# One state in eight takes its input product from GpSimd and its decay from PSUM; in the last batches four states take theirs from TensorE, and TensorE's sums move behind tiles and fills

## The reference

```
dt = softplus(x_ssm @ dt_w + dt_b);  A = -exp(A_log);  B = x_ssm @ Bp;  C = x_ssm @ Cp
state = state * exp(dt * A) + (dt * x_ssm) * B      # for every time step, channel and state
y = sum over the states of state * C                # then the D term, the gate silu(z) and Wout
```

## Time and profile before

| | us |
|---|---|
| median of the runs | 1844.28 |
| the profiled execution | 1847.7 |
| its span | 1845.9 |
| VectorE busy | 1725.2 |
| TensorE busy (modelled) | 1589.4 |
| GpSimd busy | 1371.3 |
| ScalarE busy | 1360.6 |

### The profile page before, as it was taken

One profiled execution on the slowest core, in us unless ns is written; L12 is line 12 of the kernel. 1 busy time (PEld: TensorE's weight loads), 2 busy tenths in 40 slices (PEclk: granted clock), 3 DMA queues, 4 the chain that ended last, 5 costly groups with the idle time before them and its releaser, 6 DMA issues.

```text
span 1845.9 us, 42152 instructions
## 1 busy us (share of the span) xinstructions
PE 1589.4 (86%) x12756; PEld 790.5 (43%) x12756; DVE 1725.2 (93%) x1913; ACT 1360.6 (74%) x2504; POOL 1371.3 (74%) x675
## 2 busy tenths in 40 slices
PE   1778659999999999999999999988988889888887
PEld 1544334444444444444444444443434334443343
DVE  6798559999999999999999999999999999999996
ACT  3476748878777868787878777787777687687871
POOL 5036547777777768776777777778989899888985
PEclk9688769999999999999999999999899999899998
DMA  8435565556555665567554655575456555545542
GB/s 236 148 124 187 169 161 119 127 125 175 132 126 125 150 151 126 124 146 169 120 125 125 176 125 126 124 160 129 95 120 146 138 121 103 125 118 130 129 88 64
DMA packets 202208, 249.44 MB, mean 135 GB/s; under 512 B 25939, under 2 KB 104221, under 8 KB 201949
## 3 DMA queue, kind: packets, MB, share of 16 engines
q1 hardware_dynamic: 198020, 239.78, 54.2%
q0 software_dynamic: 4096, 8.40, 1.5%
HBM read 204.00 MB, written 43.66 MB: 134 GB/s over the span
## 4 chain that ended last, share of the span: by engine, by line
PE 29%; issue 25%; DVE 20%; POOL 13%; DMA 5%; ACT 4%; DVEq 2%; SPq 1%; POOLq 0%; ACTq 0%
DVE arena L1151 11%; POOL arena L663 10%; PE ps L1329 10%; PE ps L1343 8%; DVE ps L1141 7%; DMA x_rms_by_expert<-arena,slots 4%; PE ps L1417 2%; ACT arena L883 2%; PE ps L1315 2%; POOL x_rms_by_expert L630 2%; PE ps L1393 1%; SPq L328 1%; POOL pick L587 1%; ACT arena L889 1%; DMA u_scratch<-arena 1%
## 5 line engine op out<-in xcount | busy, mean ns | idle before, releaser
L663 POOL TENSOR_TENSOR arena<-arena 128x1024 f32<-128x1024 f32 x512 | 1202.7, 2362 | 322.3 <-DVE arena L1151 286.3
L1151 DVE TENSOR_TENSOR_SCAN arena<-arena,ps 128x512 f32<-128x512 f32 x1024 | 1176.1, 1201 | 54.7 <-PE ps L1329 37.8
L883 ACT ACTIVATE arena<-arena,neg_A 128x512 f32<-128x512 f32 (+1 forms) x1024 | 671.7, 713 | 87.6 <-DVE arena L1151 86.8
L1343 PE MATMUL ps<-arena,ident 64*64 64x512 f32 x4096 | 569.4, 628 | 3.0 <-POOL arena L663 2.8
L1329 PE MATMUL ps<-arena 128*64 128x128 f32 x6144 | 437.8, 287 | 128.7 <-DVE arena L1151 119.5
L1329 PEld LDWEIGHTS ps<-arena 128*64 128x64 f32 x6144 | 342.2, 141 | 448.8 <-DVE arena L1151 286.6
L1141 DVE TENSOR_TENSOR ps<-arena,ps 128x512 f32<-128x512 f32 x640 | 406.0, 680 | 7.1 <-PE ps L1315 6.4
L889 ACT ACTIVATE arena<-ident,b_turned 128x128 f32<-128x128 f32 x768 | 242.7, 388 | 0.0
L1343 PEld LDWEIGHTS ps<-arena,ident 64*64 64x64 f32 x4096 | 110.6, 134 | 160.2 <-issue 160.2
L630 POOL DMA_INDIRECT x_rms_by_expert<-arena,slots x64 | 69.9, 1091 | 127.6 <-DVE slots L1096 89.2
L1315 PE MATMUL ps<-b_parts,pick 120*128 120x512 bf16 x320 | 124.0, 387 | 13.0 <-DVE arena L1151 12.5
(11 more groups left out here) (166 smaller groups left out, 957.1 us busy)
## 6 DMA issues: line engine op xcount, KB each, us to landing
arena<-c_scratch SPq DMA_DIRECT2D x128, 1024.0 KB, 8.7
arena<-w_routed_scaled SPq DMA_DIRECT2D x40, 256.0 KB, 5.9
arena<-in_L_ffn_W_r_dram SPq DMA_DIRECT2D x40, 256.0 KB, 8.5
arena<-w_shared_tiles SPq DMA_DIRECT2D x128, 64.0 KB, 8.0
x_rms_by_expert<-arena SPq DMA_DIRECT2D x1, 5120.0 KB, 22.4
arena<-x_rms_by_expert SPq DMA_DIRECT2D x40, 128.0 KB, 7.2
routed_by_expert<-arena SPq DMA_DIRECT2D x40, 128.0 KB, 8.3
sz_scratch<-arena SPq DMA_DIRECT2D x8, 512.0 KB, 4.6
```

Of the source, the lines that this page charges most:

```text
L663: nc.gpsimd.tensor_tensor(products[:, i % RING, :, :], states[:, i % 2, :, :], c_rows[:, i // CG, i % CG, :].unsqueeze(1).broadcast_to((P, ...
L883: nc.scalar.activation(decay[:, 2 * i + h, :], dflat[:, ds(slot + h * L, L)], ACT.Exp, scale=aflat[:, ds(col, 1)]).then_inc(s["decay_ready ...
L1151: vector.tensor_tensor_scan(states[:, i % 2, h, :], decay[:, m, :], ps[bank][:], 0.0, ALU.mult, ALU.add).then_inc(s["scanned"], 1)
L1343: ins = mm(y_ps[r][HP * h:HP * h + HP, :], ident[q, q], products[q, slot, h, :], start=False, stop=False, skip_group_check=True)
```

## The change

- `KIND` becomes a pair: DEDDEDEP for block groups, DEDDEDEE for the others. State 6 changes from D to E in both. State 7 is of a new kind P in block groups and stays E in the others. Both have four D states instead of five.
- A P state: GpSimd computes u*B into SBUF with one operation of 128x1024, issued after the product of state 1, from a row of B that a new DMA broadcasts to all partitions (256 KB, `b_row`). ScalarE writes the state's two decays into the two PSUM banks, in the slots of its order that belong to states 5 and 6; all other decays keep their place. The scan then has its decay in PSUM and u*B in SBUF.
- In the last batches a fourth state needs diagonal copies by ScalarE and fills by TensorE.
- In every slot of TensorE's queue the second fill moves behind the tiles and other work of the slot, and the sum moves behind the second fill.
- The two matmuls that open the expert sum in a batch's head are gone; the first expert matmul starts the sum. They now stand in the seven final groups (`begin_final`) and in the last group, with DMAs for xn and the gates.
- `pick` keeps one column per row of B (96x32 instead of 120x5120), and the matmul reads it with a broadcast step of 0. The projection of C and B has 128 output rows instead of 104.

The diff, cut to its core:

```
-    KIND = "DEDDEDDE"
+    KIND = ("DEDDEDEE", "DEDDEDEP")
+    P_AT = SG - 1
...
-        pick = sb("pick", [3 * SQ, SQ, P], BF16)
+        pick = sb("pick", [3 * SQ, SQ], BF16)
...
+        u_b = products[:, RING]
...
+            def load_b_row(u, g, tb):
+                if not isinstance(u, int) or u:
+                    sp.wait_ge(s["u_b_pooled"], u)
+                sp.dma_start(b_row, c_d[S:C_B_ROWS][ds(g, 1), ds(tb, L)].broadcast_to((P, L))).then_inc(s["b_row_loaded"], 16)
...
                 load_w1_shared(u, g)
                 if block:
+                    load_b_row(u, g, tb)
                     e = expert_of(u)
                     load_x_rows(u)
...
+                    if blocks and i == 1:
+                        pool.wait_ge(s["dt_u_loaded"], b * 32 + 32)
+                        pool.wait_ge(s["b_row_loaded"], (b * E + g) * 16 + 16)
+                        nc.gpsimd.tensor_tensor(
+                            u_b, u_in.rearrange("p n h t -> p (n h t)")[:, ds(slot, NH * L)].rearrange(
+                                "p (h t) -> p h t", h=NH),
+                            b_row.unsqueeze(1).broadcast_to((P, NH, L)), ALU.mult).then_inc(s["u_b_pooled"], 1)
...
+            def decay_to_psum(u, g, slot, h):
+                col = snap(g * SG + (h * S + P_AT))
+                nc.scalar.activation(ps[BANKS[True][P_AT][h]][:], dflat[:, ds(slot + h * L, L)], ACT.Exp,
+                                     scale=aflat[:, ds(col, 1)]).then_inc(s["p_decay_ready"], 1)
...
                         act.wait_ge(s["scanned"], m0 + (2 * i + h + 1))
+                        if block_before and (i, h) in ((P_AT - 2, 1), (P_AT - 1, 0)):
+                            decay_to_psum(*before, 1 - h)
+                        if KIND[block][i] == "P":
+                            continue
...
+                        if KIND[block][i] == "P":
+                            dve.wait_ge(s["u_b_pooled"], u + 1)
+                            dve.wait_ge(s["p_decay_ready"], u * NH + (h + 1))
+                            vector.tensor_tensor_scan(states[:, i % 2, h, :], ps[bank][:], u_b[:, h, :], 0.0,
+                                                      ALU.mult, ALU.add).then_inc(s["scanned"], 1)
+                            continue
...
-            def open_ffn(b, odd):
-                pe.wait_ge(s["open_loaded"], b * (16 * N_OPEN) + 16 * N_OPEN)
-                pe.wait_ge(s["xn_loaded"], max(b * 16 + 16, 32))
-                mm(ffn_ps[:], ident[:], xn_in[:, odd, :], start=True, stop=False)
-                mm(ffn_ps[:], b2_sb[:], gates_in[:], start=False, stop=False).then_inc(s["sums_opened"], 1)
+            def add_xn_b2(bank, xn):
+                mm(bank[:], ident[:], xn, start=False, stop=False, skip_group_check=True)
+                mm(bank[:], b2_sb[:], gates_in[:], start=False, stop=False, skip_group_check=True)
...
-                    for k in (HEAD_SUM_AT if head else SUM_AT).get(i, ()):
-                        if k >= 0 or not head or last is not None:
-                            ysum(n0, k)
-                    if ahead and KIND[ahead[1]] == "E":
-                        fill(*ahead, ahead_odd, 1)
                     if block:
                         if first and i == FIRST_X_AT:
                             turn_x(u)
...
+                    if ahead and KIND[ahead[3]][ahead[1]] == "E":
+                        fill(*ahead, ahead_odd, 1)
+                    for k in (HEAD_SUM_AT if head else SUM_AT).get(i, ()):
+                        if k >= 0 or not head or last is not None:
+                            ysum(n0, k)
```

215 lines of the change are left out of this document (126 added, 89 removed).

## The result

| | before | after |
|---|---|---|
| median of the runs made together, us | 1845.7 | 1834.2 |
| span of the profiled execution, us | 1845.9 | 1833.4 |
| ratio, 95% interval | | 0.9947 (0.9935 to 0.996) |

The change makes the kernel 11.5 us faster by the medians; by the ratio it is 0.5%. The forecast was 30 us faster. The time lies inside the range of 1795 to 1840 and outside the likeliest case's own of 1800 to 1829.

What follows compares the result with a forecast made beforehand. VectorE, busy 93% of the span, was taken as the bound. Gains of 12 + 15 + 2.3 + 0 + 0.8 = 30 us took 1844.3 to 1814 us, with an 8-in-10 range of 1795 to 1840.

Steps and rivals of the forecast that it cites:

- likeliest case: Whole kernel: forecast of 1814 us, own range 1800 to 1829, chance 0.73.
- GpSimd's waits in block groups: Thirty middle block groups: waits of 0.35 at states 4 and 7, group 23.89 to 23.5, 12 us gained.
- Batch 0: First two groups of batch 0: 3.4 us shorter, with 0.5 more than other batches for its longer wait.
- state P's decay is late: Rival: ScalarE's second PSUM decay comes late, 1.5 to 2 us in 40 groups; 1878 us at 1.6; chance 0.06.
- The constants: Start to first scan: smaller `pick` lets SP's stores go some 4 us earlier, VectorE's first scan 2.3 us earlier.
- the 2.29 go: Preamble: VectorE's 2.29 us wait for the scaled weights disappears, and no more than that is gained.
- Heads and second groups of batches 1 to 4: Heads 0.6 us shorter and second groups 2.3 shorter per batch; 11.6 us gained over these four batches.
- The last three batches: Final groups wait 1.5 to 2 us, six groups behind them 1.7; sum 0, between -15 and +20 us.
- The clock: TensorE behind new waits: throttled clock costs some 2 us in each of six groups, making the sum 12 us higher.
- At the end: Last group: one pair of multiplications less, 0.8 us gained after its wait.
- the last batches take it back: Rival: final groups cost 2 us more and the clock falls behind new waits, 26 us, giving 1840; chance 0.12.

Runs made afterwards that it cites:

- the third buffer: The changed kernel with a third state buffer, so scans of states 2 to 7 wait for products one state further back: 1784.8 us, ratio 0.9674.
- Another order on ScalarE: The changed kernel with group 0's P decays behind group 1's decays of states 0 and 1 and state 1's diagonal copies: 1828.3 us, ratio 0.991.
- the kernel before with the small `pick`: The kernel before with a third state buffer and `pick` cut to 40 columns: 1845.0 us, ratio 0.999.
- the one with the new order: The kernel before with only TensorE's sums and second fill moved behind each slot's other work, the fill first: 1863.2 us, ratio 1.01.
- the changed kernel with the wait last: The changed kernel with VectorE's wait for GpSimd's product placed last, directly before the state's first scan: 1819.2 us, ratio 0.9873.

## Why the prediction was wrong

**GpSimd's waits in block groups: the step that failed most (8.4 us of the missing 17.5).** The places, states 4 and 7, and the cause, the product of two states back, were right. The sizes weren't: "it waits 0.35" counted from the product's end to the scan without the instructions that stand between the wait and the scan in a loop, 0.2 us at each place. With them out of the way the waits were 0.37 and 0.25 and the group 23.40, against 23.5 forecast. The 0.1 for GpSimd's ninth operation wasn't needed: u*B takes 2.37 and its successor follows at once (744.97 to 747.29 for u*B and the start of product 2). With a group that gains 0.4 when all goes well, 0.2 twice is the whole of it. (In full, against the third buffer's 22.57: the two waits and the overlap that they lose cost 1.20, where the forecast had 0.8 with its 0.1; and a group without them is 22.57, not 22.7, because the pair of multiplications ahead of state 2 takes 1.17 instead of 1.30.) The larger miss is what the gain hung on: the forecast named the two state buffers as a rule of the code, took the two waits as a given and put no price on a third buffer, which was worth 50 us.

**Batch 0 (5.8 us).** The forecast gave its head the saving of the other heads. It had the rival "state P's decay is late" and looked for it in the loop, where the decays were in time (the second ended at 758.15, for a scan at 759.4). It wasn't worked out for the first group, where ScalarE comes out of the gelus 32 us into the group with a whole group of decays ahead of the P decays: 6.85 us. So the first group got 6.6 us longer (40.43 to 47.05, forecast 0.6 shorter), and the second 4.3 shorter (28.03 to 23.76, forecast 2.8): it waited for fills before, as the earlier trace rows show in a later batch, and waits for none now. Another order on ScalarE gets 3.2 back.

**The constants (2.8 us).** Two steps failed. GpSimd's selections did fall from 18.66 us to 0.91, and SP issued the zeros 5.2 us earlier (22.30 against 27.48), but "the 2.29 go" didn't happen: the wait is 2.42. The zeros landed no earlier (49.86 against 49.92), and the bias store's issue ended at 45.69 against 46.33. SP's long issue was read as the store's own cost, which it isn't. Second, the wait wasn't on the path. VectorE's last step before its first scan, before, after, and in the kernel before with the small `pick`:

```profile
234.04 1.22 DVE L1151 TENSOR_TENSOR_SCAN arena<-arena,ps 128x512 f32<-128x512 f32 x1 [8.20 <-POOLq L635]
```

```profile
234.54 2.33 DVE L1222 TENSOR_TENSOR_SCAN arena<-arena,ps 128x512 f32<-128x512 f32 x2 [11.98 <-POOLq L676]
```

```profile
234.47 2.33 DVE L1151 TENSOR_TENSOR_SCAN arena<-arena,ps 128x512 f32<-128x512 f32 x2 [8.03 <-POOLq L635]
```

VectorE stood 8.2 us for the end of GpSimd's scatters in the kernel before; this row was there to be read. After the change it gets there 3.3 us earlier and waits 3.8 longer; but it gets there at anything from 222.6 to 227.0 in the kernels with the change, and at 226.4 with the small `pick` alone, so the 3.3 say nothing. In all fourteen it then waited for the scatters, 4.6 to 12 us, and the first scan varies by more than the 2.8 us in question. A shorter scatter phase wasn't tried.

**Heads and second groups of batches 1 to 4.** Right in both parts: heads -2.7 (forecast -2.4), second groups -10.1 (forecast -9.2). A wait of 0.44 or 1.05 stands at state 6 of the heads (forecast 0.6), 0.62 at state 1 of the second groups and 0.20 behind it (forecast 1.4 in all). That it came through the two matmuls and not the order is argued, as said above.

**The last three batches.** The parts were near: 1.92 in final groups (forecast 1.5 to 2), plain groups 23.35 (23.3), sum +4.5 in a band of -15 to +20. Behind final groups 1.26 to 1.31 came four times, where the forecast had 1.7 six times, and the 2.8 us by which group 62 waits longer weren't in it: two misses that in part make up for each other. What it didn't do was to add the parts up the other way: two matmuls in the wrong group cost 14.6 us, and without them these batches would have gained 10.1.

**The clock.** Behind the 1.42 us of waiting TensorE kept its 2.4 GHz: the matmul took 1.10 us, not 2. Behind the longest wait, 3.97 us in group 62, it didn't: two later operations took 1.84 and 1.91 us instead of 1.02 and 1.05, and the group's granted clock is 0.94. Over the last three batches the mean rose from 0.94 to 0.98. In most plain groups it was 0.93 before, with a longest wait of TensorE of 1.97 us, and is 1.00 now, with 1.21. Here the Trainium skill's rule that idle gaps send the array back to its throttled clock (TensorE: Matmul & The Clock Gate, "HAM oscillation — how this bites in real kernels") fits group 62 and, as the forecast had it, the plain groups, but the 2 us that the forecast's working gave to each group behind a final one didn't come. Waits of 1.2 to 1.6 us don't decide it by their length: behind 1.42 us here the clock held, and behind 1.58 and 1.21 us in the tail of the kernel before it fell.

At the end the clock gave more than the change did. From 1834 to 1840 us, in the tail of the kernel before, the granted clock was 0.60, mostly the 1.2 GHz level, behind those two waits of sums for GpSimd; after the change the stretch of the projection has 1.00. A sum (1.98 against 1.09 us) and the projection make 2.7 of the 3.5 us gained at the end (0.8 forecast). The projection (four records) before, after, and in the changed kernel with the wait last:

```profile
1835.05 3.78 PE L1350 MATMUL ps<-arena,wout_sb 128*128 128x512 f32 x4 [0.86 <-DVE arena L1116]
```

```profile
1824.33 1.98 PE L1421 MATMUL ps<-arena,wout_sb 128*128 128x512 f32 x4 [0.86 <-DVE arena L1177]
```

```profile
1805.22 3.67 PE L1424 MATMUL ps<-arena,wout_sb 128*128 128x512 f32 x4 [0.86 <-DVE arena L1177]
```

The last row is of a kernel that has the whole change. Of the eleven profiled kernels with the change in them the clock fell there in this one alone; of the three without it, it held in one, the one with the new order. So these 2.7 us came often with the change but not surely, the forecast had no term for them, and as part of its result they are luck. Why the clock holds or falls there stays open.

**The rivals.** None came about as written: a bit of "the last batches take it back", through the waits and not the clock, and "state P's decay is late" in one group of forty.

## What to carry to other kernels

When an edit takes work from the engine that sets the pace, write down the distance of every buffer between it and its neighbours: what was hidden at 23.9 us a group was a wait at 22.6, and one buffer decided over 50 us where the edit alone gave 11. When a gain is a few tenths of a microsecond a turn, count the instructions between the last wait and the operation, and put the wait that comes last, last. And before a wait early in a program is priced, read the last wait of that phase; if it belongs to someone else, the early one is worth nothing.

## What the runs showed of the hardware that was not expected

- In a loop with thresholds in registers, a scan began 0.21 us behind the product's end when the waits for its other operands stood between, 0.04 us when none did; in a group with constant thresholds it was 0.03 us with them between.
- A wait of VectorE costs its length and about 0.1 us more, as operations that follow each other overlap by 0.09 us.
- SP's issue of the same store took 18.42 us, 22.05 or 4.14, and that of another 1.62 or 8.17, in different places of SP's order; what stood there was through at 45.7 to 46.8 us. The time of an issue isn't the instruction's own price.
- A broadcast's matmul whose weights are a `pick` column read with a step of 0 took 0.39 us, as with 128 stored columns before (387 and 394 ns in the two pages).
